# Split down weights kept in device memory and read back, in a kernel of two mixture-of-experts blocks around a state-space block

## Time and profile before

| | |
|---|---|
| median of three runs | 1242.63 us (1241.94 to 1242.85) |
| the profiled execution | 1242.78 us, of which the span of the instructions 1241.0 us |
| PE busy | 1233.1 us, 99% of the span, 7072 products |
| DVE busy | 1143.2 us, 92% |
| ACT busy | 1003.5 us, 81% |
| POOL busy | 447.8 us, 36% |
| granted TensorE clock | 1.00 throughout |
| mean transfer rate | 149 GB/s, 184.84 MB |
| POOL's transfers with accumulation | 252 + 99 + 21 = 372, with 53568 packets |

### The profile page before, as it was taken

How to read it: one execution, slowest core, us unless ns; L and a number is a source line. 1 busy time by engine, 2 the same in 40 slices (tenths; PEclk the granted TensorE clock), 3 DMA queues, 4 the chain that set the end, 5 groups by cost and what they waited for, 6 DMA issues and landing times.

```text
span 1241.0 us, 20186 instructions
## 1 busy us (share of the span) xinstructions
PE 1233.1 (99%) x7072; PEld 1058.0 (85%) x7072; DVE 1143.2 (92%) x1368; ACT 1003.5 (81%) x2122; POOL 447.8 (36%) x571
## 2 busy tenths in 40 slices
PE   9999999999999999999999999999999999999999
PEld 6788788888888888888888888888888888887887
DVE  6958899999999999999999999997999999978877
ACT  7678789798898898988879898797998978846664
POOL 1021134444453453453435434452444454402000
PEclk9999999999999999999999999999999999999999
DMA  7412458787788997987889797986688989932322
GB/s 227 111 26 54 104 108 173 165 170 168 162 177 166 194 186 155 201 167 168 180 182 184 167 195 161 190 182 141 128 165 169 196 170 195 182 75 43 68 52 52
DMA packets 121015, 184.84 MB, mean 149 GB/s; under 512 B 11344, under 2 KB 38096, under 8 KB 120912
## 3 DMA queue, kind: packets, MB, share of 16 engines
q0 software_dynamic: 53568, 97.54, 45.0%
q1 hardware_dynamic: 67344, 86.00, 26.2%
HBM read 83.30 MB, written 2.69 MB: 69 GB/s over the span
## 4 chain that ended last, share of the span: by engine, by line
PE 89%; DVE 4%; ACT 4%; issue 2%; DMA 1%; POOL 0%; SPq 0%; DVEq 0%; ACTq 0%; POOLq 0%
PE PS L1105 26%; PE PS L996 18%; PE PS L999 18%; PE PS L997 18%; PE PS L1101 2%; PE PS L1097 2%; PE PS L1099 2%; DVE HB L1345 1%; PE PS L1163 1%; PE PS L1148 1%; PE PS L1032 1%; DVE HL L1301 1%; PE PS L1040 1%; ACT DA L1643 1%; DMA YE<-CWD 1%
## 5 line engine op out<-in xcount | busy, mean ns | idle before, releaser
L1105 PEld LDWEIGHTS PS<-WD,HB 128*128 128x128 f32 x3200 | 393.8, 191 | 22.1 <-issue 2.0
L1105 PE MATMUL PS<-WD,HB 128*128 128x128 f32 x3200 | 395.8, 275 | 0.0
L1345 DVE TENSOR_TENSOR HB<-PS,HB 128x1024 f32<-128x1024 f32 (+1 forms) x336 | 322.7, 961 | 72.4 <-PE PS L999 56.1
L1555 ACT ACTIVATE HB<-PS 128x512 f32<-128x512 f32 x512 | 294.9, 596 | 95.7 <-PE PS L999 93.5
L1733 POOL DMA_DIRECT2D Y<-HS x252 | 222.5, 964 | 317.1 <-DMA Y<-HS 165.5
L996 PE MATMUL PS<-XH,WG 128*128 128x512 f32 x509 | 219.5, 431 | 0.3 <-ACT HB L1555 0.2
L996 PE MATMUL PS<-XH,WU 128*128 128x512 f32 x512 | 204.6, 400 | 0.5 <-DVE HB L1345 0.4
L999 PE MATMUL PS<-XH,WU 128*128 128x512 f32 x512 | 201.1, 393 | 0.0
L999 PE MATMUL PS<-XH,WG 128*128 128x512 f32 x509 | 200.8, 394 | 0.1
L997 PE MATMUL PS<-XH,WU 128*128 128x512 f32 x512 | 200.6, 392 | 0.0
L997 PE MATMUL PS<-XH,WG 128*128 128x512 f32 x509 | 199.2, 391 | 0.0
(11 more groups left out here) (164 smaller groups left out, 1573.7 us busy)
## 6 DMA issues: line engine op xcount, KB each, us to landing
BCB<-BCD SPq DMA_DIRECT2D x128, 512.0 KB, 5.2
Y<-HS POOLq DMA_DIRECT2D x252, 256.0 KB, 6.0
XT<-YE POOLq DMA_DIRECT2D x99, 256.0 KB, 5.1
YE<-CWD SPq DMA_DIRECT2D x27, 256.0 KB, 4.6
AT<-YE POOLq DMA_DIRECT2D x21, 256.0 KB, 3.3
WD<-in_L_ffn_w_down_dram SPq DMA_DIRECT2D x8, 256.0 KB, 6.2
XT<-in_L_attn_x_dram SPq DMA_DIRECT2D x7, 256.0 KB, 6.0
out_dram<-XT SPq DMA_DIRECT2D x7, 256.0 KB, 5.5
```

Source lines behind the costliest of these rows:

```text
L1105: z = pe.matmul(part(g, j), HB[:, i % NH, j * P:(j + 1) * P], WD[:, e, c, :], start=c == 0 and j == 0, stop=c == FC - 1 and j == SUB - 1)
L1345: v.tensor_tensor(H, PS[:, NG + i % 2:NG + i % 2 + n, :], H, ALU.mult).then_inc(S["v_h"], 1)
L1555: a.activation(HB[:, i % NH, :], gate(i), ACT.Silu).then_inc(S["a_sil"], 1)
```

## The change

1. Each of the 16 different pairs of down weights is split once (MADE: the first pair with these weights, ten in position 0, four in position 1, two in position 14) and then stored by SP to a tensor WDD in device memory (`wd_store`). The other 38 pairs (READ) are not split: SP reads them back (`wd_load`) into the ring.
2. The ring WDS grows from two pairs to three. A slot of the ring is free when the down products of the pair three before it are done and, if that pair was split here, its store has landed.
3. A `wd_store` stands in the list right after its `wd_lo` and waits for it on SP. A `wd_load` stands four slots ahead of its use, behind the `cw_load`s of experts that come before.
4. For the last tile, `closing` lets 2.0 us of the planner's PE clock pass after each of the two last state sums, where it went on at the next call.
5. The scratch for descriptors is 4096 bytes per partition, which with the third pair's 2048 bytes fits into SBUF.

```diff
+APART = 2.0
+WEIGHTS_RING = 3
+PAIRS_TURNED = [i for i in TURNED_SLOTS if i % PAIR == 0]
+MADE = [i for i in PAIRS_TURNED if not any(k % SLOTS == i % SLOTS for k in PAIRS_TURNED if k < i)]
+READ = [i for i in PAIRS_TURNED if i not in MADE]
...
         if t == NT - 1:
             for n in range(LAST):
                 step("s_y", n, v=1.17)
-                yield False
+                yield from until(clock["pe"] + APART)
...
+    reads = []
+
+    def weight_loads():
+
+        while reads and (asked[0] == len(TURNED) or TURNED[asked[0]] * FC + FC > reads[0] - SPLIT - PAIR - 2):
+            step("wd_load", reads.pop(0))
...
             m = nd + SPLIT
-            if m % PAIR == 0 and m in TURNED_SLOTS:
+            if m in MADE:
                 split_at[m] = split(m)
                 if m not in scalar_splits:
                     step("wd_lo", m, v=.4)
+                    step("wd_store", m)
             m -= 1
             if m in scalar_splits:
                 step("wd_lo", m, after=split_at[m], v=.35)
+                step("wd_store", m)
+            m = nd + SPLIT + PAIR
+            if m in READ:
+                reads.append(m)
             row_loads()
+            weight_loads()
...
-        WDS = sb("WDS", [P, 2, 2, PAIR, P], F32R)
+        WDS = sb("WDS", [P, WEIGHTS_RING, 2, PAIR, P], F32R)
         AT = sb("AT", [P, T])
+        WDD = nc.dram_tensor("WDD", [E, FC // PAIR, P, 2, PAIR, P], F32).ap()
...
         def wait_weights_free(eng, i):
 
-            n = TURNED_SLOTS[i]
-            if n >= 2 * PAIR:
-                eng.wait_ge(S["m_dn"], [k for k in TURNED_SLOTS if TURNED_SLOTS[k] == n - PAIR - 1][0] + 1)
+            n = pair(i) - WEIGHTS_RING
+            if n >= 0:
+                eng.wait_ge(S["m_dn"], PAIRS_TURNED[n] + PAIR)
+                if PAIRS_TURNED[n] in MADE:
+                    wait_weights_stored(eng, PAIRS_TURNED[n])
...
+                elif s[0] == "wd_store":
+                    i = s[1]
+                    wait_weights_high(wt, i)
+                    wt.wait_ge(S["v_wd"], MADE.index(i) + 1)
+                    r = pair(i) % WEIGHTS_RING
+                    sy.dma_start(WDD[i // FC % E, i % FC // PAIR], f32(WDS[:, r])).then_inc(S[f"c_ws{r}"], 16)
+                elif s[0] == "wd_load":
+                    i = s[1]
+                    wait_weights_free(wt, i)
+                    wait_weights_stored(wt, [k for k in MADE if k % SLOTS == i % SLOTS][0])
+                    r = pair(i) % WEIGHTS_RING
+                    sy.dma_start(f32(WDS[:, r]), WDD[i // FC % E, i % FC // PAIR]).then_inc(S[f"c_wl{r}"], 16)
...
-                        wait_weights_high(wt, first)
+                        if first in MADE:
+                            wait_weights_high(wt, first)
+                        else:
+                            wait_weights_read(wt, first)
...
-    nc = _bacc.Bacc("TRN2", target_bir_lowering=False, num_devices=1, dynamic_dma_scratch_size=8192)
+    nc = _bacc.Bacc("TRN2", target_bir_lowering=False, num_devices=1, dynamic_dma_scratch_size=4096)
```

More of the change, by code:

```diff
@@ L747, in macaron_program @@
             S[n] = ctx.enter_context(nc.semaphore(n))
+        for r in range(WEIGHTS_RING):
+            S[f"c_ws{r}"] = ctx.enter_context(nc.semaphore(f"c_ws{r}"))
+            S[f"c_wl{r}"] = ctx.enter_context(nc.semaphore(f"c_wl{r}"))
         for b in range(BR):
@@ L826, in wait_weights_high @@
             by_scalar = i in scalar_splits
-            same = [k for k in TURNED_SLOTS if k <= i and k % PAIR == 0 and (k in scalar_splits) == by_scalar]
+            same = [k for k in MADE if k <= i and (k in scalar_splits) == by_scalar]
             eng.wait_ge(S["a_wd" if by_scalar else "v_wh"], len(same))
@@ L840, in wait_weights_free, with wait_weights_stored, wait_weights_read @@
         def wait_weights_free(eng, i):
-            n = TURNED_SLOTS[i]
-            if n >= 2 * PAIR:
-                eng.wait_ge(S["m_dn"], [k for k in TURNED_SLOTS if TURNED_SLOTS[k] == n - PAIR - 1][0] + 1)
+            n = pair(i) - WEIGHTS_RING
[3 more added lines that the diff above has]
+                    wait_weights_stored(eng, PAIRS_TURNED[n])
+        def wait_weights_stored(eng, i):
+            r = pair(i) % WEIGHTS_RING
+            eng.wait_ge(S[f"c_ws{r}"], 16 * sum(k <= i and pair(k) % WEIGHTS_RING == r for k in MADE))
+        def wait_weights_read(eng, i):
+            r = pair(i) % WEIGHTS_RING
+            eng.wait_ge(S[f"c_wl{r}"], 16 * sum(k <= i and pair(k) % WEIGHTS_RING == r for k in READ))
         def added(g):
@@ L1091, in _ @@
                     if g in TURNED:
-                        W = WDS[:, pair(i) % 2]
+                        W = WDS[:, pair(i) % WEIGHTS_RING]
                         first = i // PAIR * PAIR
                         high = HI[:, TURNED_SLOTS[i] % HI_RING, :]
-                        wait_weights_high(wt, first)
+                        if first in MADE:
+                            wait_weights_high(wt, first)
+                        else:
+                            wait_weights_read(wt, first)
                         wait_high(wt, i)
                         pe.matmul(turned(g), W[:, 0, c % PAIR, :], high, start=c == 0, stop=False)
-                        wt.wait_ge(S["v_wd"], pair(i) + 1)
+                        if first in MADE:
+                            wt.wait_ge(S["v_wd"], MADE.index(first) + 1)
                         pe.matmul(turned(g), W[:, 1, c % PAIR, :], high, start=False, stop=False)
@@ L1307, in _ @@
                     wt.wait_ge(S[f"c_wd{i // FC % E}"], 16)
-                    v.tensor_copy(WDS[:, pair(i) % 2, 0], WD[:, i // FC % E, c:c + PAIR, :]).then_inc(S["v_wh"], 1)
+                    v.tensor_copy(WDS[:, pair(i) % WEIGHTS_RING, 0], WD[:, i // FC % E, c:c + PAIR, :]).then_inc(S["v_wh"], 1)
                 elif k == "wd_lo":
@@ L1312, in _ @@
                     wait_weights_high(wt, i)
-                    v.tensor_tensor(WDS[:, pair(i) % 2, 1], WD[:, i // FC % E, c:c + PAIR, :], f32(WDS[:, pair(i) % 2, 0]),
+                    v.tensor_tensor(WDS[:, pair(i) % WEIGHTS_RING, 1], WD[:, i // FC % E, c:c + PAIR, :], f32(WDS[:, pair(i) % WEIGHTS_RING, 0]),
                                     ALU.subtract).then_inc(S["v_wd"], 1)
@@ L1571, in _ @@
                     wt.wait_ge(S[f"c_wd{i // FC % E}"], 16)
-                    a.activation(WDS[:, pair(i) % 2, 0], WD[:, i // FC % E, c:c + PAIR, :], ACT.Copy).then_inc(S["a_wd"], 1)
+                    a.activation(WDS[:, pair(i) % WEIGHTS_RING, 0], WD[:, i // FC % E, c:c + PAIR, :], ACT.Copy).then_inc(S["a_wd"], 1)
                 elif k == "acc" and s[1] in scalar_weighs:
```

2 lines of the change are left out of this document (added).

## The result

The changed kernel took 1243.92 us (median of 20 runs, 1242.55 to 1248.19), the kernel before 1242.64 us in runs beside it: ratio 1.0015, 95% interval 1.0009 to 1.0020. By the medians it is 1.3 us slower (a ratio of 1.0010; the ratio of 1.0015 would be 1.9 us), within the 0.2% that I called no change, 0.4 us from the forecast of 1243.5 and inside the range.

A forecast was written before the change was run, and what follows sets the result against it. PE was taken to be bound by its own products, on 89% of the last-ending chain. Terms -1.2 - 0.3 + 2.4 = +0.9 us gave 1243.7 profiled, 1243.5 us as a median, range 1239.9 to 1247.2.

The forecast's parts named there:

- The sum: Whole kernel: gains of 1.2 and 0.3 us against a loss of 2.4 us, +0.9 us in all.
- the redrawn order: From slot 36 the planner's cheaper clocks place steps anew: 0.3 us gain at 160.74, 0 in the middle.
- Last positions: Positions 14 and 15: removed splits relieve three PE waits for HL, the low part of h; gain 1.2 us, 0.7 to 1.4.
- The wait at 160.74: End of position 1, PE idle 1.23 us: may go if DVE's Mamba steps are placed otherwise; gain 0.3, 0 to 1.3.
- Start: Position 0: stores on SP delay the routing-weights row for the first turned expert, and PE; loss 2.4 us, 2.1 to 4.4.
- The ring: Pair 10 first reuses a slot, pair 4's, whose store has had over 10 us to land; nothing lost.
- The reads: Read pairs land in about 6 us where 9.7 us lie between; nothing lost, ends 0 and 1 us.
- The middle: Slots 36 to 447: order drawn again, PE's work the same; 0 us, ends -2 and +3.7 us.
- Last state sums and scratch: Delayed sums near 1093 us covered by PE's products; smaller descriptor scratch not stalling POOL; nothing for either.
- The range of the forecast alone: Start costs, last positions give, rest as before: 1241.5 to 1245.5 us; chance 0.50.
- the rival that I gave 0.22: Slower: redrawn order puts long DVE steps ahead of products of h in the middle; doubled waits give 1247.2; chance 0.22.

The follow-up runs named there:

- the order of before: Changed kernel, but the planner still counts the 38 removed splits and the last-state-sums condition is undone, so only SP's list is new: 1242.47 us, ratio 1.0003.
- row-in-time kernel: Changed kernel with SP's list in position 0 reordered: two stores behind the small loads, three behind the first rows; 1243.53 us, ratio 1.0007 to the kernel before.
- its repeat: The changed kernel run and profiled again with no edit: 1244.56 us, ratio 1.0019 to the kernel before.
- half the scratch: The kernel before with 4096 bytes of transfer scratch and nothing else: 1242.10 us, ratio 1.0001.
- rows first: Changed kernel with stores moved to positions 1 and 14, 24 reads, condition undone, first two rows ahead of expert 6's loads: 1241.94 us, ratio 0.9996 to before.

## Why the prediction was right in its sum and wrong in two of its terms

The sum was +0.9 us; the medians say +1.3 beside one set of runs and +2.2 beside another. Two errors of opposite sign cancelled in it, which was luck: the start cost 1.4 us less than I said, and the redrawn order, which I had put at a gain of 0.3, cost 1.2 to 2.1.

- **Last positions, gain 1.2.** Third column: 1.0 us in every kernel with the reads, 1.3 to 1.4 with the order of before. Right, and the three waits fell to one.
- **The wait at 160.74, gain 0.3.** 0.27 us of 1.23 are left, so this place gave 1.0, in the upper part of my range; position 1 as a whole gave nothing, since all three profiles of the redrawn order lose 0.9 to 1.1 us between slots 32 and 60, with the same products of PE before both, and one of the projection's waits (0.9 us) lies there. It comes with the redrawn order, as I said: with the order of before it is still there (1.6 us of the weight load's wait).
- **Start, loss 2.4.** The mechanism held up to the row's issue, to 0.3 us: against PE, the issue moved by 2.6 us (2.15 later, and slot 12 was 0.4 earlier) where I had 2.3. I had left out that the routing weights must land, which ended last, 0.1 us behind the issue of the loads. The term was mis-sized behind it: I carried the 6.81 us under way over, and it took 5.04 and 4.73. The loss is 1.0 us by the medians of both pairs and 0.9 by the means of the first column. I took a landing time for a constant of the transfer, where it is a measure of what else is in the queues. In the kernel before, the three loads of expert 7 are issued right behind the rows, from 33.7 us on; in the change they come at 42.2. The row-in-time kernel separates the two: its row is issued at 31.96, as before, with three stores behind it and these loads at 41.5, and it lands at 36.95, after 4.99 us; with the same list and the order of before it takes 5.6. Over all profiles the row takes 4.7 to 5.6 us in the seven without weight loads right behind it and 6.05 to 7.1 in the seven with them. So the stores cost the start 2.6 us of issue and gave back 1.8 us by holding up these loads.
- **The ring, "Nothing".** True of the change, whose pairs of position 1 are read. It is not true of the ring: I reasoned from the ten microseconds that store 4 has, not from what can stand in the queue ahead of a store. With the splits of position 1 kept and stores 144 us into the kernel, it costs 0.7 us of PE's time.
- **The reads, "Nothing".** Right: no product waits for one; in the changed kernel's profile they land in 2.5 to 5.8 us, median 2.7, against 9.7 us of time (the stores in 2.0 to 7.6).
- **The middle, 0.** This is the step that failed: a redrawn order put at nothing, with ends from waits that were there before. Undoing the redrawn order gives 2.1 us, at both starts (1.2 us if the first median of the change is taken), and that is net of the 1.0 us gained at 160.74. I had sized this rival by doubling the waits for HB; those did not grow (3.0 us; 3.7 and 3.3 in the two profiles of before). What grew were waits that the kernel before scarcely had: for the step-size projection (3.1 us in eight waits of its weight loads for RM and DX, where before has 0.8 in two) and for a layernorm behind POOL's transfers. All three profiles of the redrawn order have the 3.0 to 3.1 us at the projection, none of the eleven with the old order has over 0.8; the layernorm's wait is long in one of the three, since it hangs on a landing. By the profiles the middle costs 1.0 us on the mean: 1074.9 in the second column, against 1073.9 for the nine of the old order without the ring's wait. But two of the three are the fastest executions of their runs (1242.55 of 20, 1241.82 of 11), 1.4 and 1.7 us under the medians, and just these have the short wait for the layernorm. The third has the long one and took 1244.51, with a median of 1244.56; against the order of before with the same list on SP (1242.48, median 1242.47) its second column is 2.3 us longer, nearly all of it around the layernorm: from slot 209 to 250 it takes 107.1 us, the other two 105.8, and the order of before 104.8 to 105.2. So the long wait may well be the usual case and the rest of the 2.1 us; one profile at the median does not show it.
- **Last state sums and scratch, nothing.** Both right within the noise of about a microsecond, each measured alone. The estimate from the Trainium skill ("DMA: Bandwidth & Descriptors", Terms, and SWDGE vs HWDGE vs iDMA), that the smaller area holds seven times what is open, fits the unchanged 6.0 us; it takes a packet for a descriptor, and the factor itself no run shows.
- **The range of the forecast alone**, 1241.5 to 1245.5, does not follow from its terms: their ends add up to 1242.0 (1242.6 - 1.4 - 1.3 + 2.1) and 1246.3 (1242.6 - 0.7 + 4.4). The measured times lie inside either.

So the rival that I gave 0.22, the slower one by the redrawn middle, was half true at the same time as the forecast: the redrawn order did cost, but not by long DVE steps ahead of products of h.

## What to carry to other kernels

When a planner with clocks writes the order of a kernel, taking work off an engine that is not the bound is two changes: the work that goes, and a new order everywhere behind it. Measure the first alone, by letting the planner count the removed work still; here the removal was worth 0.8 us (its interval reaches to nothing), and the new order cost 1.2 to 2.1. A transfer's time to landing belongs to its company in the queues: before a transfer is added, ask which transfer of any queue, with an engine waiting behind it, is then under way, and which transfers behind the new one in its list come later and meet others (as the row and the read at 1169 us did).

## What the runs showed of the hardware that was not expected

PE's steps of the last positions take either 2.05 or 2.08 us, for the same nine products: the product starts are 0.228 or 0.231 us apart, at a granted clock of 1.00. An execution keeps one rhythm over such a stretch: all fourteen profiles have 2.08 from slot 478 to 483, and behind the step of slot 484 (2.5 us) six have 2.05 and eight 2.08, to the last slots. From slot 485 on this makes the 0.66 us between 62.77 and 63.43 in the fourth column. The rows of L1146, first of the changed kernel, then of its repeat (min/median/max in ns):

```profile
L1146 PE MATMUL PS<-HI,WDS x108: 387/389/793, 22.5 to 1231.3; 128*128 128x512 f32 x108
```

```profile
L1146 PE MATMUL PS<-HI,WDS x108: 387/397/793, 22.6 to 1233.2; 128*128 128x512 f32 x108
```

What chooses the rhythm stays open. Second, two of the fourteen profiles (half the scratch, and rows first) reach slot 0 at 11.6 us instead of 9.5 to 9.9, and both are the slowest executions of their runs. The load of x issued at 1.22 us landed 3.07 and 3.03 us after its issue there, and in 2.1 to 2.6 us in the others; that is a part of the 2 us, and the rest is not looked into.
